# First mixture layer: ten row buffers for the expert tiles, and a new order of work within the routing slots

## The chip, the core and the metric

The kernel runs on one core of a Trainium2 chip. The metric is the device time of one execution in microseconds (us), the median of several. The core's engines are TensorE (PE in the profile; its weight loads are PEld), VectorE (DVE), ScalarE (ACT), GpSimd (POOL) and SyncE (SP), which here only issues DMAs. They run side by side and meet through semaphores.

## The reference, cut to what matters

Four layers follow one another on x, 4096 tokens (8 batches of 512) of 256 numbers, each as `x = x + layer(layernorm(x))`: attention, a mixture of experts, a Mamba block, and a second mixture. The change is in the first mixture:

```python
logits = x @ router_weight                      # 8 experts
probs = softmax(logits)
_, topk_idx = top_k(probs, 2)
local_probs = probs * one_hot(topk_idx, 8).sum(axis=1)
y1, y2 = split(einsum('th,ehf->tef', x, w1), 2) # w1: 8 x 256 x 704
o = einsum('tef,efh->teh', silu(y1) * y2, w2)   # w2: 8 x 352 x 256
out = einsum('teh,te->th', o, local_probs)
```

## The kernel before, in words

`four_phases` runs the four layers one after the other, with a barrier of all engines between them. The first mixture, `moe_swiglu_phase`, has two blocks of its own, again with a barrier between.

**The routing block** goes over the 8 batches in ten slots (`SLOTS = range(NB + 2)`). A batch passes through three slots: in slot n its layernorm, in slot n + 1 its logits and exponents, in slot n + 2 its top two experts, its places in the lists, and the scatter of its rows. So a slot s works on batches s, s - 1 and s - 2 side by side. Each engine has its own program with the slots written out in order; it takes its instructions strictly in that order, and semaphores hold it back. Beside that, in slot s the weights of expert s are split into a high and a low part, in three pieces: ACT makes the high part (`hi(s, 0..2)`, L718) and DVE the low one (`lo(s, 0..2)`, L762), which waits for the high one.

What DVE does in a slot, in order: top two of batch s - 2 (L769 to L784, waits for the exponents), statistics of batch s (L788, L791), places of batch s - 2 (L797 to L804, waits for PE's ranks), logits minus their maximum for batch s - 1 (L808, L809, waits for PE's logits), `lo(s, 0)`, the Newton step for 1/sqrt(variance) of batch s (L814 to L821), `lo(s, 1)`, `lo(s, 2)`. ACT: transposed rows out of PSUM (L725, batch s - 1), the second copy of the rows to scatter (L729, batch s - 2), `hi(s, 0)`, the first guess of the root (L735, L737), exponents (L740, batch s - 1), `hi(s, 1)`, the normalised rows (L748, batch s), `hi(s, 2)`. PE: transposes (L858, batch s - 1), ranks (L863, L866, batch s - 2), logits (L873, batch s - 1). POOL: for each batch eight scatters of 128 rows (L705) into the lists of the experts in device memory, once the places are known (`idx_ready`).

The normalised rows lie in `pay[0]`, a ring of three batches, their copy in `pay[1]`, a ring of two. Before ACT writes rows of batch n into `pay[0]` it waits until all scatters of batch n - 3 have landed (`landed(act, n - RING[0])`), before it writes the copy until those of batch n - 2 have. After the last slot DVE works out tables of tiles (L829 to L845), SP stores eight blocks of padding behind the lists (L680), and the barrier follows.

**The expert block** goes over 71 tiles of 128 rows, each of one expert; the last few are empty. In PE's slot t stand: transposes of the rows of tile t + 1 (L978), the first products of tile t (L988, with the look-up of the next tile's expert between its halves), transposes of the gated values of tile t - 1 (L996), the second product of tile t - 2 (L1006). DVE scales the outcome of tile t - 2 by its probability (L963) into `o`, a ring of three, and POOL adds it to x in device memory with an indirect DMA (L922). POOL waits there for the landing of the add two tiles earlier, and at the first tile of an expert for that of the tile just before. SP loads the rows of the tiles (L908) into `xs`, a ring of `XR6 = 6`; from the seventh tile on it first waits (L907) until the add of the tile six earlier has landed, since that add reads its row numbers from the buffer.

Of the kernel before, what the change touches and what calls it, by code (L numbers as in the profile page):

```python
# [7 lines left out]
ALU = mybir.AluOpType  # L8
# [553 lines left out]
def moe_swiglu_phase(nc, sem, A, x_io):  # L562
# [6 lines left out]
    ROW = D + 2  # L569
    XR6 = 6  # L570
    I32 = mybir.dt.int32
    with ExitStack() as ctx:
# [14 lines left out]
        w_in = [sem(f"m0_w_in{j}") for j in range(3)]  # L587
        xs_loaded = [sem(f"m0_xs_loaded{r}") for r in range(XR6)]
        passed = sem("passed")

        with ExitStack() as rctx:
# [36 lines left out]
            def batch(n):  # L628
                return n if 0 <= n < NB else None
# [14 lines left out]
            with nc.Block() as block:  # L644
# [66 lines left out]
                def _(act):  # L711
# [9 lines left out]
                    for s in SLOTS:  # L721
                        if (n := batch(s - 1)) is not None:
                            act.wait_ge(S["xT_ps"], n + 1)
                            wait(act, S["logits"], n)
                            act.activation(xT[:, :, :], f_ps[:, :, :], ACT.Copy).then_inc(S["xT_ready"], 1)  # L725
                        if (n := batch(s - 2)) is not None:
                            if n > 1:
                                landed(act, n - 2)
                            act.activation(pay[1][:, n % RING[1], :, 0:D], pay[0][:, n % RING[0], :, 0:D], ACT.Copy).then_inc(S["copy_ready"], 1)  # L729
                        if s < E:  # L730
                            hi(s, 0)
                        if (n := batch(s)) is not None:
                            act.wait_ge(S["var_ready"], n + 1)
                            wait(act, S["norm_set"], n)
                            act.activation(y0[:, :], mv[:, :, 1], ACT.Ln, bias=eps[:, :]).then_inc(S["ln_ready"], 1)  # L735
                            act.wait_ge(S["ln_ready"], n + 1)
                            act.activation(y0[:, :], y0[:, :], ACT.Exp, scale=-0.5).then_inc(S["rs_raw"], 1)  # L737
                        if (n := batch(s - 1)) is not None:
                            act.wait_ge(S["z_ready"], n + 1)
                            act.activation(p[:, n % 2, :, :], p[:, n % 2, :, :], ACT.Exp).then_inc(S["exp_ready"], 1)  # L740
                        if s < E:
                            hi(s, 1)
                        if (n := batch(s)) is not None:
                            act.wait_ge(S["norm_set"], n + 1)
                            if n >= RING[0]:
                                landed(act, n - RING[0])
                            for k in range(4):
                                last = act.activation(pay[0][:, n % RING[0], k, 0:D], x[:, n % 2, k, :], ACT.Identity, bias=nb[:, k:k + 1], scale=rs[:, k:k + 1])  # L748
                            last.then_inc(S["norm_ready"], 1)
                        if s < E:  # L750
                            hi(s, 2)

                @block.vector
                def _(dve):
# [9 lines left out]

                    for s in SLOTS:
                        if (n := batch(s - 2)) is not None:
                            now = p[:, n % 2, :, :]
# [17 lines left out]
                        if (n := batch(s)) is not None:  # L785
# [6 lines left out]
                            ins.then_inc(S["var_ready"], 1)  # L792
                        if s == 0:
                            dve.wait_ge(S["const_in"], 16 * N_CONST)
                        if (n := batch(s - 2)) is not None:
# [9 lines left out]
                        if (n := batch(s - 1)) is not None:  # L805
# [3 lines left out]
                            dve.tensor_tensor(p[:, n % 2, :, :], z_in, per_row(zmax[:, :]), ALU.subtract).then_inc(S["z_ready"], 1)  # L809
                        if s < E:  # L810
                            lo(s, 0)
                        if (n := batch(s)) is not None:
                            dve.wait_ge(S["var_ready"], n + 1)
                            steps.mark(dve.tensor_scalar(av[:, :], mv[:, :, 1], 1e-5, None, ALU.add))  # L814
                            dve.wait_ge(S["rs_raw"], n + 1)
                            wait(dve, S["norm_ready"], n)
                            steps(dve.tensor_tensor(tv[:, :], y0[:, :], y0[:, :], ALU.mult))
                            steps(dve.tensor_tensor(tv[:, :], tv[:, :], av[:, :], ALU.mult))
                            steps(dve.tensor_scalar(tv[:, :], tv[:, :], -0.5, 1.5, ALU.mult, ALU.add))
                            steps(dve.tensor_tensor(rs[:, :], y0[:, :], tv[:, :], ALU.mult))  # L820
                            dve.scalar_tensor_tensor(nb[:, :], mv[:, :, 0], -1.0, rs[:, :], ALU.mult, ALU.mult).then_inc(S["norm_set"], 1)  # L821
                        if s < E:
# [53 lines left out]
        eb = sb  # L876
        xs = eb("xs", [P, XR6, ROW])
        xsT_hi, xsT_lo = (eb(f"xsT_{q}", [P, 2, 2, P], F32R) for q in ("hi", "lo"))
# [20 lines left out]
        with nc.Block() as block:  # L899

            @block.sync
            def _(sp):
                for t in SLOTS:
                    if (q := tile(t + 2)) is not None:
                        if q >= XR6:
                            sum_landed(sp, q - XR6)
                        at = sp.value_load(first_row[0:1, q:q + 1], min_val=0, max_val=LIST)  # L907
                        sp.dma_start(xs[:, q % XR6, :], xs_d[bass.ds(at, P), :]).then_inc(xs_loaded[q % XR6], 16)  # L908

            @block.gpsimd  # L910
            def _(pool):
                for t in SLOTS:
                    if (q := tile(t - 3)) is not None:
# [3 lines left out]
                        elif q:  # L917
# [3 lines left out]
                            pool.sem_inc(passed, 1)  # L921
                        pool.indirect_dma_start(x_io, bass.IndirectOffsetOnAxis(ap=xs[:, q % XR6, D:D + 1].bitcast(I32), axis=0),  # L922
                                                o[:, q % 3, :], None, compute_op=ALU.add).then_inc(added[q % 2], 16)
# [21 lines left out]
            def _(dve):  # L945
                for t in SLOTS:
# [11 lines left out]
                    if (q := tile(t - 2)) is not None:  # L958
                        dve.wait_ge(S["o_ready"], q + 1)
                        dve.wait_ge(xs_loaded[q % XR6], 16 * (q // XR6 + 1))  # L960
                        if q > 2:
                            sum_landed(dve, q - 3)
                        dve.tensor_scalar(o[:, q % 3, :], o_ps[:, q % 2, 0:D], xs[:, q % XR6, D + 1:D + 2], None, ALU.mult).then_inc(S["o_scaled"], 1)  # L963

            @block.tensor
            def _(pe):
# [6 lines left out]
                for t in SLOTS:  # L973
                    if (q := tile(t + 1)) is not None:
                        pe.wait_ge(xs_loaded[q % XR6], 16 * (q // XR6 + 1))
                        wait(pe, S["lo_ready"], q)
                        for kt in range(2):
                            last = pe.transpose(t_ps[:, 0, kt * P:(kt + 1) * P], xs[:, q % XR6, kt * P:(kt + 1) * P], ident[:, :])  # L978
                        last.then_inc(S["xs_ps"], 1)
# [821 lines left out]
```

## Time and profile before

| | |
|---|---|
| median of 3 runs | 2495.03 us (2494.74 to 2502.99) |
| the profiled execution | 2503.31 us, of which the trace spans 2501.5 us |
| routing block in the trace | 674 to 828 us |
| expert block in the trace | 828 to 1159 us |
| busy share of the span | PE 80%, DVE 69%, POOL 58%, ACT 49% |

Lines L12 are lines of the kernel. A row of a timeline has the start, the duration, the engine, the line, the operation, what it writes and reads, how many instructions it merges, and in brackets how long the engine was idle before and who ended that. A clock of 1.00 is TensorE at full speed, 0.50 at half.

### The profile page before, as it was taken

The numbers are of one execution on the slowest core, as the hardware profiler recorded it, in microseconds if no ns is written. First come the engines' busy times: TensorE is split into PE (matmuls) and PEld (weight loads), VectorE is DVE, ScalarE is ACT, GpSimd is POOL, SyncE is SP. The second block draws the span as 40 slices with busy tenths as digits, with TensorE's granted clock in tenths as the row PEclk, the third lists the DMA queues.
The fourth block names the chain that finished last, engine by engine and source line by source line (L and its number), as shares of the span: only waits on it lengthen the run. The fifth ranks groups of instructions, "written<-read, shape, count | busy, mean of one in ns | idle before, by whom it ended". The sixth has DMA issues, their size and how long they took to land. (4 is left out here: it accounts for less than half of the span.)

```text
span 2501.5 us, 33097 instructions
## 1 busy us (share of the span) xinstructions
PE 2001.5 (80%) x10054; PEld 1180.2 (47%) x10054; DVE 1714.5 (69%) x2416; ACT 1221.1 (49%) x2476; POOL 1447.2 (58%) x1146
## 2 busy tenths in 40 slices
PE   2699999998544688883698989898989887649998
PEld 1334444433244688883334444444444443237776
DVE  4587777765165244442199999999999999945564
ACT  1176666666343222221567675666666665412332
POOL 7354444322146233332299999999989999824444
PEclk9899999999655899996888989999999998868999
DMA  4554444431253333332313030303040312011000
GB/s 88 107 108 99 105 101 102 88 83 41 70 167 122 73 61 60 62 60 57 113 40 135 17 136 17 136 17 136 19 144 30 122 66 79 1 61 34 27 29 28
DMA packets 235169, 190.05 MB, mean 76 GB/s; under 512 B 148585, under 2 KB 205553, under 8 KB 235010
## 3 DMA queue, kind: packets, MB, share of 16 engines
q1 hardware_dynamic: 221714, 170.31, 24.6%
q0 software_dynamic: 13296, 17.77, 4.0%
q8 instruction: 82, 1.34, 0.2%
q14 instruction: 77, 0.63, 0.1%
HBM read 138.53 MB, written 49.49 MB: 75 GB/s over the span
## 5 line engine op out<-in xcount | busy, mean ns | idle before, releaser
L1476 POOL TENSOR_TENSOR mb_dbu<-mb_dtu,mb_bbc 128x1024 f32<-128x1024 f32 x256 | 601.8, 2362 | 74.2 <-DVE mb_hp L1618 48.1
L318 DVE TENSOR_REDUCE at_mx<-at_s_ps 128x2 f32<-128x1024 f32 x256 | 312.5, 1224 | 116.1 <-PE at_s_ps L395 115.5
L1681 PE MATMUL mb_y_ps<-mb_hc,mb_ident 128*128 128x512 f32 x640 | 332.3, 645 | 74.2 <-DVE mb_hc L1626 74.2
L250 ACT ACTIVATE at_probs<-at_t_ps 128x512 f32<-128x512 f32 x512 | 292.1, 596 | 200.0 <-PE at_t_ps L386 194.2
L1620 DVE TENSOR_TENSOR_SCAN mb_da_ps<-mb_da_ps,mb_dbu 128x1024 f32<-128x1024 f32 x160 | 365.2, 2283 | 17.3 <-ACT mb_da_ps L1529 17.3
L386 PE MATMUL at_t_ps<-at_qst,at_kst 64*128 64x512 f32 x512 | 203.1, 488 | 47.0 <-ACT at_probs L250 42.0
L1681 PEld LDWEIGHTS mb_y_ps<-mb_hc,mb_ident 128*128 128x128 f32 x640 | 125.4, 205 | 243.2 <-issue 124.8
L922 POOL DMA_INDIRECT x<-m_o,m_xs x71 | 111.0, 1563 | 221.8 <-DMA x<-m_o,m_xs 126.0
L1482 POOL TENSOR_TENSOR mb_hp<-mb_hp,mb_cbc 128x1024 f32<-128x1024 f32 x96 | 226.8, 2362 | 0.0
L1618 DVE TENSOR_TENSOR_SCAN mb_hp<-mb_da_ps,mb_dbu 128x1024 f32<-128x1024 f32 x96 | 218.8, 2279 | 0.0
L1626 DVE TENSOR_TENSOR mb_hc<-mb_da_ps,mb_cbc 128x1024 f32<-128x1024 f32 x160 | 196.0, 1225 | 18.9 <-PE mb_y_ps L1681 1.8
L1527 ACT ACTIVATE mb_da_ps<-mb_zero 128x1 f32<-128x1 f32 x256 | 43.6, 170 | 323.3 <-DVE mb_hc L1626 272.3
L1681 PE MATMUL mb_y_ps<-mb_hp,mb_ident 128*128 128x512 f32 x384 | 196.9, 638 | 0.0
L386 PEld LDWEIGHTS at_t_ps<-at_qst,at_kst 64*128 64x128 f32 x512 | 78.0, 187 | 234.0 <-ACT at_probs L250 194.9
L395 PE MATMUL at_s_ps<-at_kst,at_qst 48*128 48x512 f32 x512 | 166.6, 448 | 13.7 <-DMA at_kst<-at_scr 8.1
L1528 ACT ACTIVATE mb_da_ps<-mb_dt,mb_a_neg 128x512 f32<-128x512 f32 x256 | 172.5, 674 | 0.0
L1529 ACT ACTIVATE mb_da_ps<-mb_dt,mb_a_neg 128x511 f32<-128x511 f32 x256 | 171.8, 671 | 0.0
L210 POOL CAST at_nm_parts<-at_nm 4x512 fp32r<-4x512 f32 x32 | 19.2, 601 | 238.1 <-ACT at_nm L263 238.1
L1103 POOL TENSOR_TENSOR m_odd<-m_odd,m_odd_in 128x256 f32<-128x256 f32 x96 | 70.8, 738 | 133.1 <-ACT m_odd_in L1161 130.1
L405 PE MATMUL at_o_ps<-at_probs,at_vau 128*32 128x512 f32 x1024 | 139.1, 616 | 0.0
L953 DVE TENSOR_TENSOR m_g<-m_g,m_y_ps 128x352 f32<-128x352 f32 x71 | 37.0, 521 | 125.7 <-ACT m_g L937 125.7
L1681 PEld LDWEIGHTS mb_y_ps<-mb_hp,mb_ident 128*128 128x128 f32 x384 | 78.5, 207 | 83.6 <-issue 79.8
(282 smaller groups left out, 4437.2 us busy)
## 6 DMA issues: line engine op xcount, KB each, us to landing
mb_bbc<-mb_scr SPq DMA_DIRECT2D x64, 512.0 KB
mb_cbc<-mb_scr SPq DMA_DIRECT2D x64, 512.0 KB, 4.7
at_qst<-at_scr SPq DMA_DIRECT2D x192, 64.0 KB, 2.4
at_kst<-at_scr SPq DMA_DIRECT2D x192, 64.0 KB, 2.3
m_xs<-m_xs_list SPq DMA_DIRECT2D x71, 129.0 KB
at_scr<-at_qk_hi SPq DMA_DIRECT2D x32, 256.0 KB
at_scr<-at_qk_lo SPq DMA_DIRECT2D x32, 256.0 KB
m_x<-x SPq DMA_DIRECT2D x16, 512.0 KB, 4.4
```

The costliest lines, as they stand in the source:

```text
L250: act.activation(probs[:, c, h, :], t_ps[:, k % 2, :], ACT.Exp, scale=SCALE).then_inc(exp_done, 1)
L318: dve.tensor_reduce(out, s_ps[:, m % 2, :, :], AX.X, ALU.max).then_inc(max_done, 1)
L386: pe.matmul(t_ps[:, k % 2, :], of_head(kst, r, h, 64, c), of_head(qst, r, h, 64), start=True, stop=True).then_inc(t_ready, 1)
L395: last = pe.matmul(s_ps[:, m % 2, a, :], of_head(qst, u % 4, h + 2 * a, 48, c), of_head(kst, u % 4, h + 2 * a, 48), start=True, stop=True)
L1476: pool.tensor_tensor(dbu[:, q % 3, :, :], dtu_2, bbc[:, 2 * p:2 * p + 2, :], ALU.mult).then_inc(S["dbu_ready"], 1)
L1482: pool.tensor_tensor(hp[:, r, :, :], hp[:, r, :, :], cbc[:, 2 * p:2 * p + 2, :], ALU.mult).then_inc(S["hp_ready"], 1)
L1528: act.activation(da_ps[:, q % 2, 0, :], dt[:, d % 2, :], ACT.Exp, scale=a_neg[:, d, 2 * p:2 * p + 1])
L1529: act.activation(da_ps[:, q % 2, 1, 1:T], dt[:, d % 2, 1:T], ACT.Exp, scale=a_neg[:, d, 2 * p + 1:2 * p + 2]).then_inc(S["da_ready"], 1)
L1618: dve.tensor_tensor_scan(hp[:, t % 3, :, :].rearrange("p j t -> p (j t)"), da, add, 0.0, ALU.mult, ALU.add).then_inc(S["scan_done"], 1)
L1620: dve.tensor_tensor_scan(da, da, add, 0.0, ALU.mult, ALU.add).then_inc(S["scan_done"], 1)
L1626: dve.tensor_tensor(hc[:, t % 2, :, :], da_ps[:, r, :, :], cbc[:, 2 * p:2 * p + 2, :], ALU.mult).then_inc(S["hc_ready"], 1)
L1681: last = pe.matmul(y_ps[:, v % 2, :], ident[:, :], src[:, j, :], start=(q == tile_first[v] and j == 0), stop=(q == tile_last[v] and j == 1))
```

## The change: what it does

The ring `xs` gets ten buffers in place of six. In the routing slots, on DVE the Newton step of batch s with `lo(s, 0)` ahead of it comes before the places of batch s - 2 and the logits of batch s - 1. On ACT the copy of batch s - 2 and the exponents of batch s - 1 come after the normalised rows of batch s, ahead of `hi(s, 2)`. DVE's wait for the constants moves from slot 0 to slot 2. No arithmetic instruction is added or taken out.

```diff
-    XR6 = 6
+    XS = 10
@@ ACT, one routing slot
-                        if (n := batch(s - 2)) is not None:
-                            if n > 1:
-                                landed(act, n - 2)
-                            act.activation(pay[1][:, n % RING[1], :, 0:D], pay[0][:, n % RING[0], :, 0:D], ACT.Copy).then_inc(S["copy_ready"], 1)
                         if s < E:
                             hi(s, 0)
...
-                        if (n := batch(s - 1)) is not None:
-                            act.wait_ge(S["z_ready"], n + 1)
-                            act.activation(p[:, n % 2, :, :], p[:, n % 2, :, :], ACT.Exp).then_inc(S["exp_ready"], 1)
                         if s < E:
                             hi(s, 1)
...
                             last.then_inc(S["norm_ready"], 1)
+                        if (n := batch(s - 2)) is not None:
+                            if n > 1:
+                                landed(act, n - 2)
+                            act.activation(pay[1][:, n % RING[1], :, 0:D], pay[0][:, n % RING[0], :, 0:D], ACT.Copy).then_inc(S["copy_ready"], 1)
+                        if (n := batch(s - 1)) is not None:
+                            act.wait_ge(S["z_ready"], n + 1)
+                            act.activation(p[:, n % 2, :, :], p[:, n % 2, :, :], ACT.Exp).then_inc(S["exp_ready"], 1)
                         if s < E:
                             hi(s, 2)
@@ DVE, one routing slot
+                        if s == 2:
+                            dve.wait_ge(S["const_in"], 16 * N_CONST)
...
                             ins.then_inc(S["var_ready"], 1)
-                        if s == 0:
-                            dve.wait_ge(S["const_in"], 16 * N_CONST)
+                        if s < E:
+                            lo(s, 0)
+                        if (n := batch(s)) is not None:
+                            dve.wait_ge(S["var_ready"], n + 1)
...
+                            dve.scalar_tensor_tensor(nb[:, :], mv[:, :, 0], -1.0, rs[:, :], ALU.mult, ALU.mult).then_inc(S["norm_set"], 1)
                         if (n := batch(s - 2)) is not None:
                             dve.wait_ge(S["ranks"], n + 1)
...
                             dve.tensor_tensor(p[:, n % 2, :, :], z_in, per_row(zmax[:, :]), ALU.subtract).then_inc(S["z_ready"], 1)
-                        if s < E:
-                            lo(s, 0)
...
@@ the expert block (the same in PE's, POOL's and DVE's programs)
-                        if q >= XR6:
-                            sum_landed(sp, q - XR6)
+                        if q >= XS:
+                            sum_landed(sp, q - XS)
                         at = sp.value_load(first_row[0:1, q:q + 1], min_val=0, max_val=LIST)
-                        sp.dma_start(xs[:, q % XR6, :], xs_d[bass.ds(at, P), :]).then_inc(xs_loaded[q % XR6], 16)
+                        sp.dma_start(xs[:, q % XS, :], xs_d[bass.ds(at, P), :]).then_inc(xs_loaded[q % XS], 16)
```

## Rows read from the trace of the kernel before

**Rows 1.** Busy time by stretch: length, each engine's busy us, clock, DMA.

```profile
718.30:779.30 61.00, 30.73 (x136) 28.76 (x136) 36.77 (x161) 27.84 (x52) 36.32 (x41) 0.50 0.59 175
836.00:1131.00 295.00, 260.40 (x1759) 239.98 (x1758) 126.49 (x339) 87.38 (x273) 103.14 (x66) 1.00 0.36 60
```

**Rows 2.** Waits in the expert block: who, for whom, us, times, longest.

```profile
PE m_t_ps L978 <- DMA m_xs<-m_xs_list: 56.8, 32, 23.4
...
SPq L907 <- DMA x<-m_o,m_xs: 220.6, 64, 12.5
```

**Rows 3.** Timeline of PE in the expert block, the transposes alone.

```profile
845.26 0.38 PE L978 MATMUL m_t_ps<-m_ident,m_xs 128*128 128x128 f32 x2
849.41 0.44 PE L978 MATMUL m_t_ps<-m_ident,m_xs 128*128 128x128 f32 x2 [0.43 <-DMA m_xs<-m_xs_list]
...
1018.17 0.38 PE L978 MATMUL m_t_ps<-m_ident,m_xs 128*128 128x128 f32 x2
1021.73 0.39 PE L978 MATMUL m_t_ps<-m_ident,m_xs 128*128 128x128 f32 x2
...
1130.90 0.44 PE L978 MATMUL m_t_ps<-m_ident,m_xs 128*128 128x128 f32 x2
```

**Rows 4.** Timeline of POOL and SP in the expert block: first add, seventh load, last adds.

```profile
842.69 1.62 POOL L922 DMA_INDIRECT x<-m_o,m_xs  x1 [23.13 <-DVE m_o L963]
...
847.35 0.34 SPq L908 DMA_DIRECT2D m_xs<-m_xs_list  x1
...
1146.30 1.56 POOL L922 DMA_INDIRECT x<-m_o,m_xs  x1 [2.91 <-DMA x<-m_o,m_xs]
```

**Rows 5.** Timeline of routing slot 3 before the change, all engines.

```profile
718.34 1.40 DVE L788 BATCH_NORM_STATS2 m_stats<-m_x 128x6 f32<-128x256 f32 x4
718.48 0.65 PE L863 MATMUL m_r_ps<-m_both,m_tri 128*128 128x40 f32 x2 [3.22 <-issue]
720.63 3.56 PE L873 MATMUL m_l_ps<-m_rw,m_xT 128*128 128x8 f32 x16
721.56 0.17 DVE L803 CAST m_pos<-m_pos_f 128x8 int32<-128x8 f32 x1
722.51 0.98 POOL L705 DMA_INDIRECT m_xs_list<-m_pay,m_pos  x1 [4.03 <-DVE m_pos L803]
724.46 0.19 DVE L809 TENSOR_TENSOR m_p<-m_l_ps,m_zmax 128x32 f32<-128x32 f32 x1
724.56 0.88 DVE L762 TENSOR_TENSOR m_w_lo<-m_raw,m_w_hi 128x704 fp32r<-128x704 f32 x1
724.68 0.23 ACT L740 ACTIVATE m_p<-m_p 128x32 f32<-128x32 f32 x1 [3.96 <-DVE m_p L809]
726.22 0.16 DVE L821 SCALAR_TENSOR_TENSOR m_nb<-m_mv,m_rs 128x4 f32<-128x4 f32 x1
726.42 2.08 ACT L748 ACTIVATE m_pay<-m_x,m_nb,m_rs 128x256 f32<-128x256 f32 x4 [0.83 <-issue]
728.40 0.92 ACT L718 ACTIVATE m_w_hi<-m_raw 128x512 fp32r<-128x512 f32 x2
729.35 1.02 DVE L762 TENSOR_TENSOR m_w_lo<-m_raw,m_w_hi 128x512 fp32r<-128x512 f32 x2 [2.17 <-ACT m_w_hi L718]
731.48 1.05 ACT L729 ACTIVATE m_pay<-m_pay 128x1024 f32<-128x1024 f32 x1
733.41 0.33 POOL L698 COPY m_pay<-m_ids 128x4 int32<-128x4 int32 x2
733.61 1.40 DVE L788 BATCH_NORM_STATS2 m_stats<-m_x 128x6 f32<-128x256 f32 x4
```

**Rows 6.** Timeline of the end of the routing block.

```profile
806.99 0.19 DVE L797 TENSOR_TENSOR m_spot<-m_r_ps,m_run 128x32 f32<-128x32 f32 x1 [2.40 <-issue]
...
815.05 10.12 SPq L680 DMA_DIRECT2D m_xs_list<-m_pad  x8
...
828.18 5.90 SPq L908 DMA_DIRECT2D m_xs<-m_xs_list  x6
```

More of the change, by code:

```diff
@@ L587, in moe_swiglu_phase @@
         w_in = [sem(f"m0_w_in{j}") for j in range(3)]
-        xs_loaded = [sem(f"m0_xs_loaded{r}") for r in range(XR6)]
+        xs_loaded = [sem(f"m0_xs_loaded{r}") for r in range(XS)]
         passed = sem("passed")
@@ L792, in _ @@
                             ins.then_inc(S["var_ready"], 1)
-                        if s == 0:
-                            dve.wait_ge(S["const_in"], 16 * N_CONST)
+                        if s < E:
+                            lo(s, 0)
+                        if (n := batch(s)) is not None:
+                            dve.wait_ge(S["var_ready"], n + 1)
+                            steps.mark(dve.tensor_scalar(av[:, :], mv[:, :, 1], 1e-5, None, ALU.add))
+                            dve.wait_ge(S["rs_raw"], n + 1)
+                            wait(dve, S["norm_ready"], n)
+                            steps(dve.tensor_tensor(tv[:, :], y0[:, :], y0[:, :], ALU.mult))
+                            steps(dve.tensor_tensor(tv[:, :], tv[:, :], av[:, :], ALU.mult))
+                            steps(dve.tensor_scalar(tv[:, :], tv[:, :], -0.5, 1.5, ALU.mult, ALU.add))
+                            steps(dve.tensor_tensor(rs[:, :], y0[:, :], tv[:, :], ALU.mult))
+                            dve.scalar_tensor_tensor(nb[:, :], mv[:, :, 0], -1.0, rs[:, :], ALU.mult, ALU.mult).then_inc(S["norm_set"], 1)
                         if (n := batch(s - 2)) is not None:
@@ L809, in _ @@
                             dve.tensor_tensor(p[:, n % 2, :, :], z_in, per_row(zmax[:, :]), ALU.subtract).then_inc(S["z_ready"], 1)
-                        if s < E:
-                            lo(s, 0)
[L812 to L821, printed above, removed]
                         if s < E:
@@ L876, in moe_swiglu_phase @@
         eb = sb
-        xs = eb("xs", [P, XR6, ROW])
+        xs = eb("xs", [P, XS, ROW])
         xsT_hi, xsT_lo = (eb(f"xsT_{q}", [P, 2, 2, P], F32R) for q in ("hi", "lo"))
@@ L921, in _ @@
                             pool.sem_inc(passed, 1)
-                        pool.indirect_dma_start(x_io, bass.IndirectOffsetOnAxis(ap=xs[:, q % XR6, D:D + 1].bitcast(I32), axis=0),
+                        pool.indirect_dma_start(x_io, bass.IndirectOffsetOnAxis(ap=xs[:, q % XS, D:D + 1].bitcast(I32), axis=0),
                                                 o[:, q % 3, :], None, compute_op=ALU.add).then_inc(added[q % 2], 16)
@@ L959, in _ @@
                         dve.wait_ge(S["o_ready"], q + 1)
-                        dve.wait_ge(xs_loaded[q % XR6], 16 * (q // XR6 + 1))
+                        dve.wait_ge(xs_loaded[q % XS], 16 * (q // XS + 1))
                         if q > 2:
                             sum_landed(dve, q - 3)
-                        dve.tensor_scalar(o[:, q % 3, :], o_ps[:, q % 2, 0:D], xs[:, q % XR6, D + 1:D + 2], None, ALU.mult).then_inc(S["o_scaled"], 1)
+                        dve.tensor_scalar(o[:, q % 3, :], o_ps[:, q % 2, 0:D], xs[:, q % XS, D + 1:D + 2], None, ALU.mult).then_inc(S["o_scaled"], 1)
             @block.tensor
@@ L974, in _ @@
                     if (q := tile(t + 1)) is not None:
-                        pe.wait_ge(xs_loaded[q % XR6], 16 * (q // XR6 + 1))
+                        pe.wait_ge(xs_loaded[q % XS], 16 * (q // XS + 1))
                         wait(pe, S["lo_ready"], q)
                         for kt in range(2):
-                            last = pe.transpose(t_ps[:, 0, kt * P:(kt + 1) * P], xs[:, q % XR6, kt * P:(kt + 1) * P], ident[:, :])
+                            last = pe.transpose(t_ps[:, 0, kt * P:(kt + 1) * P], xs[:, q % XS, kt * P:(kt + 1) * P], ident[:, :])
                         last.then_inc(S["xs_ps"], 1)
```

## The prediction

> **What bounds the kernel now.** I read the busy time by stretch first, then the waits of the two blocks that the diff touches, then timelines of single slots. The layers are cut off from each other by barriers, so a saving inside the first mixture comes off the end one for one, and the chain that ended last (all in the fourth layer) is no help.
>
> In the expert block PE is busy 260 of 295 us at full clock [rows 1]; no other engine is above half. But PE waited there for tile rows 32 times, 56.8 us in all, 23.4 of them the wait for the very first tile: 33.4 us of true stalls. And SP, which loads the rows, waited for a landed add at 64 of its 65 loads from the seventh on, 220.6 us [rows 2]. So the loads are late because their buffers are not free. The loop closes so: the add of tile q - 6 starts about 2.0 us after PE has left slot q - 4; SP issues the load 4.66 us after the add started (842.69 to 847.35) [rows 4]; the rows come about 2.1 us later (PE's transposes of that tile started at 849.41, the end of its first stall) [rows 3]. That is 8.7 us to fit into the two PE slots q - 3 and q - 2, so a slot can't fall below some 4.35 us on average. Observed: the transposes from tile 5 (845.26) to tile 70 (1130.90) are 65 slots in 285.6 us, 4.39 us each [rows 3]. The bound is the ring, not PE.
>
> In the routing block the period of a slot is 15.27 us (718.34 to 733.61), the same to 0.02 us for slots 2 to 7, with no engine near full and the clock at its lower level (0.50) [rows 1, 5]. The ring there, read row by row from the end of the top two: PE's ranks (718.48 to 720.6), PE's logits (to 724.2), DVE's logits less maximum (to 724.65), low part and Newton step (to 726.38), ACT's normalised rows (726.42, 2.08), ACT's third high part (0.92), DVE's third low part (729.35, 0.94), and the top two (730.3 to 733.6) [rows 5]. Every link is a wait or an engine's program order. The block's end hangs on DVE's places of the last batch (806.99), the tables, SP's eight pad stores (815.05, 10.12 us) and the barrier (828.18) [rows 6], not on POOL's last scatter.
>
> **The change part by part.**
>
> *Ten buffers.* A load of tile q now waits for the add of tile q - 10. The same 8.7 us then have six slots instead of two: 21.4 us even at 3.57 us a slot. These stalls go completely, with 12 us to spare. What is late next is PE itself: two transposes, 12 first products, 3 transposes, 9 second products. Where two slots in a row had no stall the second shows that rate: 1018.17 to 1021.73 is 3.56 us [rows 3]; over the 15 such slots of the trace I get 3.55 to 3.87, mean 3.68, and the long ones still carry a look-up that hadn't run ahead. POOL's adds need to keep pace: an add holds POOL 1.56 us and lands at most 2.9 us later (the last adds follow one another 4.47 us apart, each waiting for the one before) [rows 4]. POOL waits for the add two tiles back: 4.5 us against 7.1 us for two slots, free. At the seven first tiles of an expert it waits for the tile before, 4.5 us against a slot of 3.6; POOL is late there by 0.9 us and catches up (I saw intervals of 2.60 and 3.11 us after such tiles), and `o` with three buffers gives DVE 4 us of slack before it would feel it. So the slot ends at 3.57 if all is hidden, and at 3.68 with POOL always a little behind plus 8 x 0.9 us if it never caught up (3.79). I take 3.65. Saving: 65 x (4.39 - 3.65) = 48.4 us; bounds 65 x (4.39 - 3.57) = 53.6 and, if only the recorded idle goes, 33.4. The last four adds are one chain of 4.47 us links before and after; I take 0.5 us off for POOL starting it late. SP's first burst is ten loads instead of six, four more at 1.18 us, all behind the first tile's: nothing.
>
> *Order in the routing slots.* The end of the top two of slot s is zero. DVE goes on with statistics and aggregation (1.40 and 0.38, 1.8 us), low part 0 and Newton step: in [rows 5] these took 724.56 to 726.38, 1.8 us. With semaphores 3.75. Before, this waited for PE's logits (6.2 us). ACT then: rows 2.08, copy 1.05, exponents 0.23, third high part 0.92; DVE: third low part 0.94, top two 3.3 [rows 5]. With the gaps between engines (0.05 to 0.1 each, as now) 8.85 us from the start of ACT's rows to the next zero. Unhindered period: 12.6 us. PE's ranks and logits (done at 5.8) and DVE's subtraction (at 6.25) lie beside ACT's rows and copy, which end at 6.95; PE leaves the ring. High part 1 on ACT (0.8 us, at 2.4) fits before the rows, low part 1 on DVE before low part 2.
>
> But ACT's rows of batch n also wait until the scatters of batch n - 3 have landed, and everything from the copy to the next top two is now queued behind that wait on ACT. Before, it cost nothing: the eight scatters of slot s took 722.51 to 733.41, 10.9 us [rows 5], a whole slot before the rows that needed the buffer. Now the places come later in the slot (after Newton: at 4.7 instead of 3.3 us), and the slot is shorter. Places at 4.7, POOL starts 0.8 later, 10.9 of issue, landing L: the buffer is free at 16.4 + L after the zero of slot s - 1, and the rows would like to start at one period + 3.75. Landing of a scatter is not shown by itself. From below it is over 0, from above the adds' 2.9 us; I take 2.9, the nearest row. The ring then runs over two slots: 8.85 + 16.4 + 2.9 = 28.15 us for two, 14.1 each, alternating about 12.65 (the rows find the buffer free) and 15.5 (they wait for it).
>
> Step by step: slot 1 has no copy and its Newton step moves ahead of the logits, which brings the first top two forward by 2.5 us (both_ready at 700.6 instead of 703.15). Slot 2 is unhindered: zero of slot 3 at 713.25 instead of 718.3 (5.1 us gained). Slots 3, 5 and 7 are hindered (15.5), 4 and 6 are not (12.65), zero of slot 8 at 785.05 instead of 794.75: 9.7 us. From there the block runs as before: the last two slots have no rows to normalise, and POOL's last scatter ends some 8 us ahead of the barrier. Bounds: with L = 0 it is some 17 us, with L = 5 some 3. The wait for the constants in slot 0 hides nothing: rows of batch 0 wait for ACT's high part 1, whose data comes at 684.2 either way.
>
> Here the row shows that the eight issues take 10.9 us where eight of 0.97 and gaps of 0.30 would be 10.2: some issues took 1.2 to 1.4 us, those beside DVE's low parts. The Trainium skill (SBUF — State Buffer, in its box on DVE and SWDGE descriptors) says that GpSimd can be shut out of a port it shares with VectorE while it writes descriptors, and so the whole scatter is held up. With DVE denser in the new slot that rule would lengthen the issue; by the rows of this case the stretch is 0.7 us a batch, and twice that would add 0.35 us a slot. The same skill (DMA: Bandwidth & Descriptors, Anatomy of one DMA) puts the fixed cost of a DMA at about 2.0 us, mostly the write receipt; with L = 2.0 the saving of the routing block would be an estimated 12 us instead of 9.7.
>
> **Sum.** 48.4 - 0.5 + 9.7 = 57.6 us. The profiled execution took 2503.31 us, so its like would take 2445.7. It stands 8.3 us above the median of the runs, which also show both values (2494.74 and 2502.99); I set the sum against the median: 2495.0 - 57.6 = 2437 us.
>
> **The rivals.**
>
> *A, the landing wait doesn't bind* (scatters land in about 1 us or POOL issues faster): every slot 12.6, the routing block saves 17 us. For: POOL's scatter packets are sparse. Against: POOL's issue alone is 10.9 of 12.6 us. Time 2495 - 48 - 17 = 2430.
>
> *B, the landing wait eats the new order* (issue stretched to 12 us and landing over 5): slots stay near 15.3, the gain of the first ones is given back, only ten buffers pay. Time 2495 - 48 = 2447.
>
> *C, PE's slot doesn't get to its best pace*: stalls go, but slots keep 3.88 us, which is 285.6 less 33.4 over 65, as look-ups stay exposed or POOL's adds set the pace. 33.4 + 9.7 = 43 us, time 2452.
>
> *D, slower: the clock.* PE would be busy nearly without a break for 240 us. It has 1.00 now, with stalls in between; in the routing block it is at 0.50 [rows 1]. If the granted clock dropped in the expert block to the lower of its two levels, a slot would be up to 2 x 3.57 = 7.1 us. It decides when more than a quarter of the slots run so (3.65 + 3.5 f above 4.39 + 0.15); at half of them the block loses 65 x 1.0 us, time 2495 + 65 - 10 = 2550. Against: nothing in 295 us of this block shows a dip.
>
> *E, the change doesn't do what it says*: the loads are late for another reason than their buffers. SP's 64 waits speak against it [rows 2]. Then only the 10 us of the routing block remain: 2485, within 0.5%.
>
> **How the numbers follow.** Forecast 0.57, A 0.12, B 0.13, C 0.13, D 0.02, E 0.03. From A with the best slot (71 us) to C without part of the routing gain (37 us), the range is 2425 to 2458. A change of under 0.5% (12.5 us) can't be told from none here, since single runs differ by 8 us. Faster 0.95, same 0.03, slower 0.02.
>
> **What would show it.** In the trace after: no PE wait for tile rows past the first tile; 65 slots in some 237 us; adds 3.6 to 3.7 us apart except at the starts of experts (4.5). SP's waits stay, since it now runs ahead and waits for a buffer anyway. Routing: rows of batch 1 start near 693 instead of 696; slots alternate 12.6 and 15.5; ACT idle before L748 in slots 3, 5, 7 with a DMA as its cause; PE's ranks and logits no longer end anyone's long wait; expert loads start near 818. Wrong if the slots stay at 15.3 or all are at 12.6, if PE's slot is above 3.9 us, or if its clock leaves 1.00.

## The result, and the profile after

| | before | after | ratio |
|---|---|---|---|
| median, us | 2496.25 (2494.74 to 2502.99, 4 runs) | 2425.8 (2421.97 to 2427.32, 4 runs) | 0.971 [0.9689, 0.9732] |
| profiled execution, us (span) | 2503.31 (2501.5) | 2427.32 (2425.5) | |

The change takes 70.5 us off by the medians, 76.0 us between the two profiled spans. The forecast was 57.6, and by the medians the saving is just past the favourable end of the stated range (2425, some 70 us off). The barriers let the span be cut into pieces (at the first statistics of the routing block, the first tile load, and the first load of the next layer), so every microsecond has a place:

| stretch, us | before | after | difference | forecast |
|---|---|---|---|---|
| attention, to the first statistics (code untouched) | 678.88 | 673.79 | -5.1 | 0 |
| routing block | 149.30 | 134.84 | -14.5 | -9.7 |
| expert block | 331.08 | 276.55 | -54.5 | -47.9 |
| everything behind | 342.2 | 340.3 | -1.9 | 0 |

The last column adds to 57.6. The 5.1 us of attention are not the change's: over the 13 profiled executions of this study, all with the same attention code, that stretch ends anywhere between 666.35 and 681.67 us.

**Expert block.** The busy time by stretch, columns as in [rows 1]; routing slots 3 to 7, then 230 us of the expert block:

```profile
706.30:777.00 70.70, 39.52 (x177) 37.23 (x177) 45.48 (x201) 34.52 (x65) 48.49 (x56) 0.50 0.58 179
820.00:1050.00 230.00, 230.00 (x1693) 228.63 (x1692) 122.18 (x328) 83.81 (x263) 100.00 (x64) 1.00 0.44 73
```

PE, busy 260 of 295 us before [rows 1], is now busy 230.00 of 230.00 at clock 1.00. The waits (who, for whom, us, times, longest), 800 to 1100 us, beside [rows 2]:

```profile
PE m_t_ps L978 <- DMA m_xs<-m_xs_list: 23.1, 1, 23.1
...
SPq L907 <- DMA x<-m_o,m_xs: 159.1, 61, 8.7
```

One wait for rows is left, the first tile's; the 33.4 us of stalls are gone. SP still waits for landed adds, 61 times, and it costs nothing: it asks for a buffer up to 8.7 us before it is free, and the rows are there before PE all the same. A long wait on a queue's engine can say that it has run ahead, not that it holds anyone up. PE's transposes, as in [rows 3]:

```profile
826.63 0.38 PE L978 MATMUL m_t_ps<-m_ident,m_xs 128*128 128x128 f32 x2
830.17 0.38 PE L978 MATMUL m_t_ps<-m_ident,m_xs 128*128 128x128 f32 x2
...
1056.45 0.38 PE L978 MATMUL m_t_ps<-m_ident,m_xs 128*128 128x128 f32 x2
```

From tile 5 (826.63) to tile 70 (1056.45) the 65 slots take 229.8 us, 3.536 us each, against 4.39 before: 55.8 us. The block's start gives 0.9 us back (the granted clock reaches 1.00 about a slot later than before) and its tail 0.4.

**Routing block.** Slot 3 of the kernel after, to be read beside [rows 5]. It is one in which the rows wait for scatters:

```profile
706.29 1.40 DVE L790 BATCH_NORM_STATS2 m_stats<-m_x 128x6 f32<-128x256 f32 x4
708.58 3.56 PE L873 MATMUL m_l_ps<-m_rw,m_xT 128*128 128x8 f32 x16
709.64 0.16 DVE L806 SCALAR_TENSOR_TENSOR m_nb<-m_mv,m_rs 128x4 f32<-128x4 f32 x1
710.01 0.99 POOL L705 DMA_INDIRECT m_xs_list<-m_pay,m_pos  x1 [0.30 <-issue]
712.40 0.19 DVE L821 TENSOR_TENSOR m_p<-m_l_ps,m_zmax 128x32 f32<-128x32 f32 x1
713.86 2.07 ACT L741 ACTIVATE m_pay<-m_x,m_nb,m_rs 128x256 f32<-128x256 f32 x4 [4.52 <-DMA m_xs_list<-m_pay,m_pos]
715.84 1.04 ACT L746 ACTIVATE m_pay<-m_pay 128x1024 f32<-128x1024 f32 x1
716.79 0.21 ACT L749 ACTIVATE m_p<-m_p 128x32 f32<-128x32 f32 x1
716.91 0.92 ACT L718 ACTIVATE m_w_hi<-m_raw 128x512 fp32r<-128x512 f32 x2
717.86 1.02 DVE L762 TENSOR_TENSOR m_w_lo<-m_raw,m_w_hi 128x512 fp32r<-128x512 f32 x2 [4.47 <-ACT m_w_hi L718]
722.11 1.40 DVE L790 BATCH_NORM_STATS2 m_stats<-m_x 128x6 f32<-128x256 f32 x4
```

The normalisation is set at 709.8, 3.5 us after the slot's start; the rows could begin, but ACT sits idle for 4.52 us in all, until a DMA: the scatters of three batches earlier, whose buffer the rows take. About 0.5 us of that it would have waited for DVE anyway, so the DMA costs some 4.0 us. PE's logits (708.58, 3.56) and DVE's subtraction (712.40) lie beside that. In the slots around it the rows start as soon as DVE's normalisation is set (ACT is idle 0.50 us until then); slots 5 and 7 wait for the scatters again:

```profile
694.49 1.40 DVE L790 BATCH_NORM_STATS2 m_stats<-m_x 128x6 f32<-128x256 f32 x4
698.05 2.08 ACT L741 ACTIVATE m_pay<-m_x,m_nb,m_rs 128x256 f32<-128x256 f32 x4 [0.50 <-DVE m_nb L806]
700.03 1.04 ACT L746 ACTIVATE m_pay<-m_pay 128x1024 f32<-128x1024 f32 x1
...
740.94 2.07 ACT L741 ACTIVATE m_pay<-m_x,m_nb,m_rs 128x256 f32<-128x256 f32 x4 [4.05 <-DMA m_xs_list<-m_pay,m_pos]
...
767.22 2.08 ACT L741 ACTIVATE m_pay<-m_x,m_nb,m_rs 128x256 f32<-128x256 f32 x4 [3.25 <-DMA m_xs_list<-m_pay,m_pos]
```

Slots 2 to 7 take 11.80, 15.82, 11.72, 15.28, 11.80 and about 14.5 us, where before each took 15.27; slots 0 and 1 are 3.5 us shorter together. The last scatter of the batch in question had ended its issue at 711.00, 738.55 and 765.62; the rows began at 713.86, 740.94 and 767.22. The landing thus took 2.86, 2.39 and 1.60 us behind the issue, less each time.

### The profile page after: what moved, and what is told of

Read it like the earlier page. It is cut to its first block and busy times, and to the rows that moved or that the text cites. A ratio compares the mean times of both kernels' runs of the same rounds, so it can differ in the third digit from the quotient of the medians.

```text
span 2425.5 us, 33097 instructions
## 1 busy us (share of the span) xinstructions
PE 1973.4 (81%) x10054; PEld 1174.3 (48%) x10054; DVE 1711.0 (71%) x2416; ACT 1220.4 (50%) x2476; POOL 1445.0 (60%) x1146
## 5 line engine op out<-in xcount | busy, mean ns | idle before, releaser
L395 PE MATMUL at_s_ps<-at_kst,at_qst 48*128 48x512 f32 x512 | 166.8, 448 | 13.1 <-DMA at_kst<-at_scr 10.2
```

The lines of the kernel that those rows point to most:

```text
L395: last = pe.matmul(s_ps[:, m % 2, a, :], of_head(qst, u % 4, h + 2 * a, 48, c), of_head(kst, u % 4, h + 2 * a, 48), start=True, stop=True)
```

## The experiments

Each run's before is the kernel before on the same chip. "Routing" and "expert" are the lengths of the two blocks in that kernel's profiled execution, cut as above.

**The two parts alone.** Kernel before with ten buffers; kernel after with six:

```
-    XR6 = 6
+    XR6 = 10
```

> The kernel before with ten row buffers, old order in the routing slots. My theory: the two parts of the change add up, since a barrier lies between them. Routing slots stay 15.27 us apart; in the expert block PE's wait for tile rows is only that for the first tile, 65 slots take 3.54 us each as in the changed kernel (55.8 us less), the block as a whole is 54 to 55 us shorter: some 2441 us beside 2496. Rival: the buffers gain less by themselves because part of the gain in the expert block came from the scatters or loads of the routing block ending in another pattern; then the slots are above 3.6 us here.

```
-    XS = 10
+    XS = 6
```

> The changed kernel with six row buffers, so the order in the routing slots alone. My theory: the routing block (first statistics to first tile load) is 14.5 us shorter (134.8 us, not 149.3), slots alternate 11.8 and 15.3 to 15.8, the expert block has its stalls back and takes 4.39 us a slot: some 2482 us beside 2496. Rival: the places of the last batches come later than POOL can use, and the gain of the order shows only with the buffers: then under 8 us.

| | after | before | ratio | routing | expert |
|---|---|---|---|---|---|
| buffers alone | 2443.39 | 2502.85 | 0.978 [0.9746, 0.9815] | 148.46 | 275.57 |
| order alone | 2488.19 | 2502.85 | 0.9949 [0.9924, 0.9973] | 134.95 | 333.93 |

The waits of PE in the expert block, buffers alone first:

```profile
PE m_t_ps L978 <- DMA m_xs<-m_xs_list: 22.9, 1, 22.9
```

and order alone:

```profile
PE m_t_ps L978 <- DMA m_xs<-m_xs_list: 57.2, 36, 23.1
```

Each part moves its own block and leaves the other as it was, within 3 us. Buffers alone give the 3.536 us slot; order alone keeps one of 4.427 (before 4.39), with a clock of 0.91 instead of 1.00 in one stretch (840 to 860 us). The medians give 59.5 and 14.7 us, 74.1 together, beside some 70 for both at once: additive within what single runs differ by.

**The changed kernel again**, on the chip of the runs with eight products, a fourth payload buffer and moved padding:

> The changed kernel again, as the yardstick for the runs beside it on the same chip. Every theory: 2.8% to 3% under the kernel before, routing block 134.8 us, 65 expert slots of 3.54 us.

2430.18 against 2500.45, 0.9709 [0.9666, 0.9752]; routing 134.95, expert 276.39. The blocks repeat to 0.2 us where the whole differs by 4.

**How many buffers.** The kernel after with `XS = 7`, `XS = 5`, and later `XS = 8`:

> The changed kernel with seven row buffers instead of ten. My theory of the ring: from the end of the product of tile q - XS to its add (2.0 us), the landing and the next load (4.66) and the load itself (2.1) are 8.7 us, and they have XS - 4 slots. With seven that is 10.6 us at 3.54 us a slot, 1.9 us to spare; at the seven first tiles of an expert the add starts some 1.5 us late, which still fits. So hardly any stall: PE's waits for rows past the first tile under 5 us, a time within 3 us of ten buffers (2426). Rival: a ring gives only in proportion, or late adds eat the slack each time: then 3.7 us a slot or more, 2436 or above.

> The changed kernel with five row buffers. By the same ring the 8.7 us have one slot, so a slot of PE is 8.7 us, 65 of them 565 us in place of 230: some 2760 us. Rival: the ring of six was bound by something else that happens to be 4.35 us (an add every 4.4 us, the landing): then five buffers cost much less, some 5 to 6 us a slot, 2520 to 2590.

> The changed kernel with eight row buffers. With five and six buffers a ring turn took 13.2 to 13.9 us over XS - 3 slots (6.97 and 4.43 us a slot), with seven it would be 3.3 to 3.5 us, just under PE's 3.54, and late adds at the first tiles of an expert broke through in some places (3.65 us on average). My theory now: with eight a turn has five slots, 17.7 us, over 3.5 us to spare, more than an add is late: no slot over 3.6 us, 3.54 on average, expert block 276 us as with ten. Rival: it is the run of tiles after an expert's first, several late adds in a row, that seven couldn't take; then eight still shows a few slots of 3.8 us or more and the block is above 278 us.

| buffers | time, us (before beside it) | expert | slot |
|---|---|---|---|
| 5 | 2659.25, one run (2502.85) | 504.33 | 6.97 |
| 6 | 2488.19 (2502.85) | 333.93 | 4.427 |
| 7 | 2436.91 (2502.85), 0.9746 [0.971, 0.9782] | 283.01 | 3.645 |
| 8 | 2425.09, one run (2512.43) | 279.0 | 3.564 |
| 10 | 2430.18 (2500.45) | 276.39 | 3.536 |

With five, the slots alternate between 5.0 and 8.7 us (PE's transposes):

```profile
903.04 0.69 PE L978 MATMUL m_t_ps<-m_ident,m_xs 128*128 128x128 f32 x2 [4.89 <-DMA m_xs<-m_xs_list]
908.13 0.39 PE L978 MATMUL m_t_ps<-m_ident,m_xs 128*128 128x128 f32 x2
916.79 0.69 PE L978 MATMUL m_t_ps<-m_ident,m_xs 128*128 128x128 f32 x2 [4.95 <-DMA m_xs<-m_xs_list]
```

Part of that is not the ring but PE's clock. Two neighbouring first products right behind the stall, and two of the next slot:

```profile
904.11 0.49 PE L988 MATMUL m_y_ps<-m_w_lo,m_xsT_hi 128*128 x1
904.40 0.49 PE L988 MATMUL m_y_ps<-m_w_hi,m_xsT_hi 128*128 x1
...
909.00 0.32 PE L988 MATMUL m_y_ps<-m_w_hi,m_xsT_lo 128*128 x1
909.16 0.33 PE L988 MATMUL m_y_ps<-m_w_lo,m_xsT_hi 128*128 x1
```

They start 0.29 us apart, then 0.16. From 830 to 1040 us the granted clock is 0.85 on average with five buffers, beside 1.00 with ten. So PE's slot behind a stall of 4.9 us takes 5.09 us (903.04 to 908.13) instead of some 3.7.

The prediction's loop (8.7 us over XS - 4 slots) gives 8.7 us a slot at five; measured are 6.97. It left out the link that closes it: PE's own work in the slot that produces the sum. With it a turn is 3.6 to 3.8 + 2.0 + 4.66 + 2.1, some 12.4 us, over XS - 3 slots. Measured are 3 x 4.39 = 13.2 before, 3 x 4.427 = 13.3 with order alone, and 2 x 6.97 = 13.9 with five. Single turns close link by link. With five, from 903.04 to 916.79: PE 5.09, then 2.08 to the add, 4.59 to the load, 1.99 to the rows, 13.75 us; at full clock that would be an estimated 12.4. Before, from the stall that ends at 1014.30 to the one that ends at 1027.23: 3.87, 2.08, 4.94 and 2.04, 12.93 us, over three slots. The two forms agree at six buffers (4.35 and 4.1 beside 4.39) and not at five or seven, so the fit of the first form at six was a coincidence. With seven buffers the turn fits in four slots (14.2 us at 3.56), but only just. One of its transposes, some tiles behind the start of an expert:

```profile
894.75 0.44 PE L978 MATMUL m_t_ps<-m_ident,m_xs 128*128 128x128 f32 x2 [0.31 <-DMA m_xs<-m_xs_list]
```

At an expert's start an add waits for the one before and the turn is longer, so some slots after it reach 4.03 to 4.71 us. Five waits for rows remain (25.5 us with the first tile's). That eight would be as good as ten was half right: no slot reaches 3.8 us, but every one is 0.03 us longer than with ten. Seven buffers show the same 3.56 in their undisturbed slots, and so do six (the shortest slots before are 3.55 to 3.57). No wait in the trace accounts for it; the 0.03 us is spread over the products of a slot. It stays open.

**Is PE alone the bound at ten buffers?** Eight first products a tile instead of twelve (the low part of the rows times the high part of the weights is left out of the sum):

```
-                            parts = [(xt, w, kt) for kt in range(2) for xt, w in ((xsT_hi, w1_hi), (xsT_lo, w1_hi), (xsT_hi, w1_lo))]
+                            parts = [(xt, w, kt) for kt in range(2) for xt, w in ((xsT_hi, w1_hi), (xsT_hi, w1_lo))]
...
-                                last = pe.matmul(y_ps[:, q % 2, half, 0:F], xt[:, q % 2, kt, :], rhs, start=(m == 0), stop=(m == 5))
+                                last = pe.matmul(y_ps[:, q % 2, half, 0:F], xt[:, q % 2, kt, :], rhs, start=(m == 0), stop=(m == 3))
```

> The changed kernel without the four products of the low part of the rows (xsT_lo with w1_hi) in the expert block, 8 instead of 12 first products a tile; it leaves out that part of the sum. My theory: with ten buffers PE alone sets the slot of 3.54 us, so it falls by four products of 0.16 us to 2.9 us, 42 us over 65 slots. Rival: the adds are the next bound close behind (POOL's starts are mostly 3.66 to 3.7 us apart, made good by a few of 1.9 to 3.3): then the slot stays above 3.3 us.

One run: 2400.1 (before 2500.45); expert 242.09. Most slots take 2.87 to 2.90 us, which is 3.536 less 4 products at 0.16, so PE alone did set the slot. The mean is 3.00, since at expert starts the next bound appears, DVE's scaling waiting for a landed add (waits 830 to 1000 us, then the instruction itself, then the stretch):

```profile
DVE m_o L963 <- DMA x<-m_o,m_xs: 20.6, 26, 2.1
```

```profile
900.65 0.48 DVE L963 TENSOR_SCALAR m_o<-m_o_ps,m_xs 128x256 f32<-128x256 f32 x1 [0.62 <-DMA x<-m_o,m_xs]
```

```profile
820.00:1000.00 180.00, 177.68 (x1314) 173.32 (x1314) 110.42 (x297) 78.40 (x241) 87.52 (x56) 0.99 0.53 87
```

The chain of adds could thus have kept up with slots of about 3.0 us, some 0.5 below what PE needs.

**Which order does the work in the routing block?** DVE's new order with ACT's old one, and the reverse:

```
+                        if (n := batch(s - 2)) is not None:
...
+                            act.activation(pay[1][:, n % RING[1], :, 0:D], pay[0][:, n % RING[0], :, 0:D], ACT.Copy).then_inc(S["copy_ready"], 1)
                         if s < E:
                             hi(s, 0)
...
+                        if (n := batch(s - 1)) is not None:
...
+                            act.activation(p[:, n % 2, :, :], p[:, n % 2, :, :], ACT.Exp).then_inc(S["exp_ready"], 1)
                         if s < E:
                             hi(s, 1)
```

> The changed kernel with ACT's old order (copy first, exponents before the second high part and the normalised rows), DVE's new one. My theory: ACT's rows now wait behind the exponents, which wait for DVE's logits at 6.1 us after the end of the top two: exponents 0.2, high part 0.8, rows 2.1, high part 0.9, low part 0.9, top two 3.3: slots of 14.3 to 14.5 us, no wait for a landing; routing block some 143 us. Rival: moving the Newton step is all that matters and ACT's order is of no account: then slots alternate 11.8 and 15.8 as in the changed kernel and the block has 135 us.

```
-                        if s < E:
-                            lo(s, 0)
-                        if (n := batch(s)) is not None:
-                            dve.wait_ge(S["var_ready"], n + 1)
...
                             dve.tensor_tensor(p[:, n % 2, :, :], z_in, per_row(zmax[:, :]), ALU.subtract).then_inc(S["z_ready"], 1)
                         if s < E:
+                            lo(s, 0)
+                        if (n := batch(s)) is not None:
+                            dve.wait_ge(S["var_ready"], n + 1)
...
```

> Ten buffers, ACT's new order, DVE's old one. My theory: the Newton step is done 8.0 us after the end of the top two as before, and now the copy and the exponents (1.3 us) stand between ACT's rows and the third high part: slots of 16.5 us, slower than before by 1.2 us each; routing block some 156 us. Rival: ACT's order alone helps a little, since the copy leaves the head of the slot: under 149 us.

| | time, us | routing | slot |
|---|---|---|---|
| both orders old (the run with buffers alone, its before 2502.85) | 2443.39 | 148.46 | 15.27 |
| DVE new only (before 2498.1) | 2436.33, one run | 142.72 | 14.28 |
| ACT new only (before 2498.1) | 2456.49, one run | 155.45 | 16.32 |
| both new (before 2500.45) | 2430.18 | 134.95 | 11.8 to 16.1 |

Both came out within 0.6 us of what was expected of the block. With DVE's order alone, ACT's exponents stay ahead of its rows and hold them until the logits are there:

```profile
712.13 1.40 DVE L790 BATCH_NORM_STATS2 m_stats<-m_x 128x6 f32<-128x256 f32 x4
...
718.48 0.23 ACT L740 ACTIVATE m_p<-m_p 128x32 f32<-128x32 f32 x1 [3.96 <-DVE m_p L821]
...
719.29 2.06 ACT L748 ACTIVATE m_pay<-m_x,m_nb,m_rs 128x256 f32<-128x256 f32 x4
...
726.42 1.40 DVE L790 BATCH_NORM_STATS2 m_stats<-m_x 128x6 f32<-128x256 f32 x4
```

With ACT's order alone, rows, copy and exponents all stand behind a normalisation that DVE still computes after the logits:

```profile
720.65 1.40 DVE L788 BATCH_NORM_STATS2 m_stats<-m_x 128x6 f32<-128x256 f32 x4
...
728.73 2.08 ACT L741 ACTIVATE m_pay<-m_x,m_nb,m_rs 128x256 f32<-128x256 f32 x4 [5.02 <-DVE m_nb L821]
...
731.65 0.21 ACT L749 ACTIVATE m_p<-m_p 128x32 f32<-128x32 f32 x1
...
736.98 1.40 DVE L788 BATCH_NORM_STATS2 m_stats<-m_x 128x6 f32<-128x256 f32 x4
```

Half of the reordering costs 7 us (155.45 against 148.46); the other half gains 5.7; the two together gain 13.5. The gain belongs to neither alone.

**Is it the scatters' buffer that lengthens every second slot?** A fourth payload buffer:

```
-            RING = (3, 2)
+            RING = (4, 2)
```

> The changed kernel with four batches in the ring of normalised rows (RING = (4, 2)), so that ACT's rows of batch n wait for the scatters of batch n - 4. My theory: the slots of 15.8, 15.3 and 14.6 us are long only by that wait (ACT idle 4.52, 4.05 and 3.25 us before L741). It goes: all slots 11.8 us. POOL needs 10.3 to 11.4 us of issue and 0.65 us of copies a batch, so it is now level with the slots and its last scatter, not the padding, may end the block: routing block 125 to 127 us instead of 134.8, 8 to 10 us off, some 2417 beside 2426. Rival: the landing was only where the wait was booked, and DVE or POOL holds the period (a ring through the places, POOL and the ids): then slots stay over 13 us and less than 3 us is gained.

2420.16 against 2500.45, 0.967 [0.9629, 0.9711]; routing 124.43, 10.4 us less than with three, expert 276.33. Slot 3 there:

```profile
713.07 1.40 DVE L790 BATCH_NORM_STATS2 m_stats<-m_x 128x6 f32<-128x256 f32 x4
716.63 2.08 ACT L741 ACTIVATE m_pay<-m_x,m_nb,m_rs 128x256 f32<-128x256 f32 x4 [0.50 <-DVE m_nb L806]
717.79 0.32 POOL L698 COPY m_pay<-m_ids 128x4 int32<-128x4 int32 x2
724.80 1.40 DVE L790 BATCH_NORM_STATS2 m_stats<-m_x 128x6 f32<-128x256 f32 x4
729.52 0.32 POOL L698 COPY m_pay<-m_ids 128x4 int32<-128x4 int32 x2
```

ACT's rows wait for no DMA any more and slots 2 to 6 take 11.72 to 11.81 us. That settles the mechanism. The lines also show what is next: POOL's batches follow one another at 11.73 us too (717.79 to 729.52), eight issues and two copies with no gap over 0.31 us. DVE's and ACT's chain and POOL's issue now need the same time.

**What ends the routing block?** The fourth buffer, and half of the padding stores issued from ACT's queue instead of SP's:

```
-                    for e in range(E):
+                    for e in range(E // 2):
...
+                    act.wait_ge(S["tables"], 1)
+                    for e in range(E // 2, E):
+                        at = act.value_load(pad_row[0:1, e:e + 1], min_val=0, max_val=LIST - P)
+                        act.dma_start(xs_d[bass.ds(at, P), :], pad[:, :]).then_inc(S["pads_stored"], 16)
```

> As the kernel with four batches in the ring, and four of the eight padding stores issued from ACT's queue instead of all from SP. My theory: the stores then end some 4.5 us earlier, but POOL's last scatters end the block, so it gains 0 to 2 us on the kernel with four batches alone (routing block 124 to 126). Rival: the chain of tables and padding still ends the block there: then 4 us more, routing block 121 to 122.

```profile
780.34 4.17 ACTq L755 DMA_DIRECT2D m_xs_list<-m_pad  x4
780.44 3.96 SPq L680 DMA_DIRECT2D m_xs_list<-m_pad  x4
...
784.75 0.96 POOL L705 DMA_INDIRECT m_xs_list<-m_pay,m_pos  x1 [0.30 <-issue]
...
795.70 10.29 SPq L912 DMA_DIRECT2D m_xs<-m_xs_list  x10
```

The padding is issued by 784.5 and half as long, but the first expert load still goes out at 795.70. 2416.91, 0.9672 [0.9631, 0.9713], is not distinguishable from the fourth buffer alone; its routing block is even 2.2 us longer (126.59). What releases the block stands in the queue instructions at its end (duration ns min/median/max, first and last start), this kernel:

```profile
L644 POOLq DRAIN  x1: 5293/5293/5293, 789.4 to 789.4; - x1
L644 SPq DRAIN  x1: 7/7/7, 789.2 to 789.2; - x1
```

POOL's queue drains for 5.29 us, to 794.7, after its last scatters have landed (the program waits for them first). The kernel before:

```profile
L644 POOLq DRAIN  x1: 5293/5293/5293, 821.6 to 821.6; - x1
L644 SPq DRAIN  x1: 7/7/7, 827.2 to 827.2; - x1
```

And the kernel after:

```profile
L644 POOLq DRAIN  x1: 5293/5293/5293, 802.4 to 802.4; - x1
L644 SPq DRAIN  x1: 7/7/7, 806.2 to 806.2; - x1
```

Before, POOL was done at 826.9 and SP at 827.2, a tie. After, POOL ends at 807.7 and SP at 806.2: POOL's scatters now end the block, by 1.5 us. The 2.2 us that moved padding loses to the fourth buffer alone are 1.1 us in slot 0, which varies by 1.6 us over these runs, and 0.9 us behind the last scatter: POOL's drain begins 3.7 us after the end of the last issue (785.7), beside 2.8 us. Whether two queues of padding beside it slow that landing was not tested.

**The best version** of these is the kernel after with the fourth payload buffer: in one series 2420.16 against 2430.18, and 10.4 us off the routing block in the trace. Moving padding adds nothing to it.

## Why the prediction was right or wrong

- *Stalls go with ten buffers, SP's waits stay*: right, by the one wait left and the 61 of SP. Rival E is out.
- *The loop's arithmetic*: wrong in form. It said 8.7 us over XS - 4 slots; it is about 12.4 to 13.9 over XS - 3. It fell at five and seven buffers. The conclusion for ten held, since both forms leave room there.
- *PE's slot after, 3.65 us*: the step that failed. It is 3.536, and 65 x 0.114 = 7.4 us are the larger half of the miss. The prediction took the 15 slots without a stall, at 3.55 to 3.87, and leaned towards their mean. The long ones were not samples of the pace to come: PE's register look-up was exposed there because a stall before had kept PE's queue from running ahead. In 836 to 1131 us of the kernel before, weight loads of the first products wait for "issue" 46 times, 11.3 us in all, and never after; in the slot that begins at 1014.30 the seventh first product, right behind the look-up, starts 0.29 us after the sixth (1015.41, 1015.70) instead of 0.16. That the stall is what exposes the look-up is argued from this, not shown by a run. It accounts for some 5.8 of the 7.4 us (3.65 against the undisturbed 3.56). The other 1.6 are the 0.03 us a slot between six, seven or eight buffers and ten, which the trace before could not show: even its shortest slot, 3.55, was above the new mean. The POOL-bound it also feared never touched PE: adds are 2.8 to 4.0 us apart, 4.4 to 5.5 at an expert's start, then 1.9 to 2.4 to catch up. The run with eight products shows how much room POOL had.
- *The routing ring and the landing wait*: the mechanism was right (PE leaves the ring, the slots alternate, ACT is idle on a DMA in slots 3, 5 and 7). The fourth buffer proves it. Rival A, in which nothing binds, is wrong although its 2430 us is nearer to the time than 2437: a time alone doesn't choose between mechanisms.
- *Its sizes*: a pair of slots was put at 28.15 us and is 27.6, 27.0 and 26.3. In the pair only two terms were off. From the rows to the next start it is 8.2 us instead of 8.85 (713.86 to 722.11 is 8.25), 1.9 us over three pairs. That term was a sum of durations plus gaps, but start to start on one engine is less than the duration: the rows of 2.08 us begin at 698.05 and the copy at 700.03, 1.98 later, and the exponents of 0.21 are followed by the high part after 0.12. The landing was put at 2.9 and took 2.86, 2.39 and 1.60, 1.9 us less in all, of which slightly longer issues took 0.3 back. Together 3.5 us. The unhindered slot is 11.8 us instead of 12.65, but that alone only moves time from one slot of a pair to the other. Slots 0 and 1 gained 3.5 instead of 2.5; the tail 0.3 against none. Together 4.8 of 14.5.
- *POOL's issue beside DVE*: a batch's issues take 10.2 to 11.4 us while the weights are split, about the 10.9 of before, and single issues up to 1.70 us (708.00) start beside DVE's low part 0 (708.01). So DVE's denser slot cost POOL little, as bounded. The Trainium skill's rule (SBUF — State Buffer, the box on SWDGE descriptors) is stated for VectorE operations in a two-port mode, with an fp32 `tensor_copy` as its example; the low parts are `tensor_tensor`s, so the prediction stretched it. No run here takes DVE's low parts away, so what lengthens these issues was not shown.
- *The fixed cost of a DMA*: the last scatter of a batch landed 2.86, 2.39 and 1.60 us after its issue ended. The Trainium skill (DMA: Bandwidth & Descriptors, Anatomy of one DMA) says about 2.0; by it each pair of slots would have been 0.9 us shorter than forecast. Measured they were 0.0, 0.5 and 1.3 us shorter by this term. Neither the page's figure nor the adds' 2.9 fits all three; the value 2.9 was right for the first only.
- *The tail hangs on SP's padding, POOL 8 us ahead*: wrong. The 8 us were counted from the end of the issue. Landing and the drain of 5.29 us come after it, and before the change the two were 0.3 us apart. It cost almost nothing here since everything shifted together (the tail is 0.3 us shorter), but a step that moves padding would have been priced wrongly, as the run on it shows.
- *The clock*: 1.00 through 230 us of unbroken matmuls. Rival D is out. The lower level came where PE had stalled: with five buffers, behind pauses of 4.9 us, products were 0.29 us apart for about 3 us and then 0.16 again; with order alone in one stretch, behind stalls of 1.2 and 1.9 us; before the change, with stalls of at most 2.5 us from 840 us on, nowhere.

The miss between spans is then 76.0 - 57.6 = 18.4 us: 6.6 in the expert block (7.4 of pace less 0.8 at start and tail), 4.8 in the routing block, 5.1 + 1.9 in code that the change doesn't touch. The 11.4 us of the first two are the prediction's. By the medians the miss is 12.9 us (70.5 - 57.6), so these 11.4 are most of it.

## What to carry to other kernels

When a stall is to go, read the pace to come from what the engine is working on (count x pitch), or from the shortest unstalled slots, not from their mean: slots behind a stall still pay for its shadow. Build a ring from start-to-start distances, include the work of the slot that closes it, and try the formula on a second buffer count before trusting a fit at one. When a run with fewer buffers stalls longer, read its clock too: part of its turn may be slower work. A queue's last DMA is not its end: landing and drain come behind it, and two ends 0.3 us apart can change places when something else is edited.

## What was not expected of the hardware

- The DRAIN of POOL's queue at the end of the routing block takes 5.29 us, the same in each kernel read here, though all scatters had landed. At the end of the expert block, behind 71 adds, it is 3.45 us. SP's takes 7 ns.
- With six, seven or eight row buffers the undisturbed slots of the expert block are 0.03 us longer than with ten, with no wait to show for it. Open.
- The landing of a scatter behind its issue is not one number: 2.86, 2.39 and 1.60 us in slots 3, 5 and 7 of the kernel after, and 3.16, 2.53 and 1.85 in its second profile. In slot 7 SP loads no more weights; whether that is the reason was not tested.
- The unchanged attention stretch varies over 15 us between executions, while the blocks behind it repeat to 0.2 us in two profiles of the changed kernel. Cutting the span at barriers made the two parts of this change readable; the difference of two spans alone would not have.
